# A MoE tail routed in two halves: centred router scores, slots by expert and rank, first rows gathered as products end

## What is computed

```python
x = x + (gelu(h2 @ w1 + b1) @ w2 + b2)      # end of the second stage
hidden = _layernorm(x)                      # (x - m) / sqrt(v + eps)
router_logits = hidden @ w_router           # 512 x 8
top_w, top_i = top_k(router_logits, 2)
top_w = softmax(top_w)
for ei in range(8):
    hmid = silu(hidden @ w0[ei]) * (hidden @ w1[ei])
    out = out + gating[:, ei:ei + 1] * (hmid @ wo[ei])
x = x + out
```

## Time and profile before

| | |
|---|---|
| time, 3 runs | 670.28 us median (668.91 to 671.87) |
| the profiled execution | 669.52 us, span 666.9 us |
| PE busy | 637.5 us (96%) |
| DVE, ACT, POOL busy | 414.5, 371.1, 245.4 us |
| mean granted TensorE clock | 0.991 of full |
| PE's share of the chain that ended last | 78% |

### The profile page before, as it was taken

How to read it: one execution, slowest core, us unless ns; L and a number is a source line. 1 busy time by engine, 2 the same in 40 slices (tenths; PEclk the granted TensorE clock), 3 DMA queues, 4 the chain that set the end, 5 groups by cost and what they waited for, 6 DMA issues and landing times.

```text
span 666.9 us, 10258 instructions
## 1 busy us (share of the span) xinstructions
PE 637.5 (96%) x3720; PEld 525.0 (79%) x3721; DVE 414.5 (62%) x691; ACT 371.1 (56%) x523; POOL 245.4 (37%) x170
## 2 busy tenths in 40 slices
PE   8989999999989999889999999699999999999994
PEld 8867888888867888767888887577888888888883
DVE  7775767658667455567794446661882735753766
ACT  4589998979963344431332443322882736745750
POOL 4059986879883132250000050160022020220233
PEclk9999999999999999999999999789999999999999
DMA  9515544452222413230265962138696573991915
GB/s 327 209 64 198 198 159 166 139 169 96 93 80 71 188 63 128 94 99 31 70 246 157 408 235 77 54 126 300 232 374 228 164 276 118 348 377 45 354 69 184
DMA packets 51846, 116.98 MB, mean 175 GB/s; under 512 B 5208, under 2 KB 5208, under 8 KB 48736
## 3 DMA queue, kind: packets, MB, share of 16 engines
q1 hardware_dynamic: 47360, 106.51, 45.5%
q10 hardware_dynamic: 3168, 5.77, 2.6%
q0 software_dynamic: 1280, 4.20, 1.9%
HBM read 102.31 MB, written 14.16 MB: 175 GB/s over the span
## 4 chain that ended last, share of the span: by engine, by line
PE 78%; DVE 7%; issue 5%; POOL 4%; ACT 4%; DMA 1%; SPq 0%; DVEq 0%; ACTq 0%; POOLq 0%
PE bank L1391 19%; PE bank L1392 18%; PE bank L1393 18%; PE bank L1405 5%; PE bank L1456 3%; POOL nat_lo L478 3%; PE bank L1457 2%; PE bank L1424 2%; PE bank L1425 2%; POOL slots_x L538 1%; PE bank L1819 1%; ACT nat_hi L595 1%; PE bank L1441 1%; PE bank L1632 1%; ACT ct_hi L562 1%
## 5 line engine op out<-in xcount | busy, mean ns | idle before, releaser
L478 POOL TENSOR_TENSOR nat_lo<-raw,nat_hi 128x512 fp32r<-128x512 f32 x104 | 136.2, 1347 | 42.3 <-ACT nat_hi L595 42.1
L526 POOL TENSOR_TENSOR e_lo<-e_raw,e_hi 128x2048 fp32r<-128x2048 f32 x9 | 41.6, 4620 | 221.5 <-ACT e_hi L751 221.5
L871 DVE TENSOR_TENSOR ct_lo<-bank,ct_hi 128x512 fp32r<-128x512 f32 x96 | 65.9, 689 | 33.3 <-ACT ct_hi L562 32.5
L1391 PE MATMUL bank<-w_hi,turned 128*128 128x512 f32 x176 | 70.1, 398 | 1.5 <-DVE turned L1309 1.4
L1393 PE MATMUL bank<-w_hi,turned 128*128 128x512 f32 x176 | 68.7, 391 | 0.0
L1392 PE MATMUL bank<-w_lo,turned 128*128 128x512 f32 x176 | 68.7, 391 | 0.0
L595 ACT ACTIVATE nat_hi<-raw 128x512 fp32r<-128x512 f32 x104 | 64.7, 630 | 0.0
L562 ACT ACTIVATE ct_hi<-bank 128x512 fp32r<-128x512 f32 x96 | 56.9, 596 | 9.0 <-PE bank L1405 6.8
L1391 PE MATMUL bank<-e_hi,turned 128*128 128x512 f32 x144 | 59.0, 409 | 1.5 <-issue 1.5
L1405 PE MATMUL bank<-ident,raw 128*128 128x128 f32 x384 | 57.7, 273 | 0.3
L1392 PE MATMUL bank<-e_lo,turned 128*128 128x512 f32 x144 | 56.9, 395 | 0.0
(11 more groups left out here) (257 smaller groups left out, 1426.2 us busy)
## 6 DMA issues: line engine op xcount, KB each, us to landing
raw<-in_ctx_dram SPq DMA_DIRECT2D x24, 1024.0 KB, 5.0
w_raw<-in_L_ffn_w_dram SPq DMA_DIRECT2D x24, 1024.0 KB, 5.3
e_raw<-in_L_ffn_wo_dram SPq DMA_DIRECT2D x16, 1024.0 KB, 8.0
w_raw<-in_L_attn_w_dram SPq DMA_DIRECT2D x8, 1024.0 KB, 5.2
e_raw<-in_L_ffn_w_dram SPq DMA_DIRECT2D x8, 1024.0 KB, 7.8
slots_x<-zeros SPq DMA_DIRECT2D x1, 4096.0 KB, 15.9
slots_y<-zeros SPq DMA_DIRECT2D x1, 3840.0 KB, 25.6
vectors<-slots_x ACTq DMA_DIRECT2D x11, 256.0 KB, 5.0
```

The costliest lines, as they stand in the source:

```text
L478: nc.gpsimd.tensor_tensor(nat_lo[:, j, :], raw[b % 2][:, j, :], nat_hi[:, j, :].bitcast(f32), ALU.subtract).then_inc(nat_lo_ready, 1)
L526: nc.gpsimd.tensor_tensor(e_lo[j][:, :, :], e_raw[j][:, :, :], e_hi[j][:, :, :].bitcast(f32), ALU.subtract).then_inc(e_lo_ready[j], 1)
L871: nc.vector.tensor_tensor(ct_lo[:, n % CR, :], src, ct_hi[:, n % CR, :].bitcast(f32), ALU.subtract).then_inc(t_lo, 1)
L1391: nc.tensor.matmul(dst, lh, rh, start=first and k == 0, stop=False)
```

## The change

1. The router's weights are centred (each column's mean over the 512 inputs is taken out, by 4 matmuls and one DVE instruction in the eighth feature step, `n == 8` and `n == 9`), so scores come from the unnormalised `xt`; `gap` is multiplied by `rstd` afterwards.
2. Tiles 0 and 1 are turned, scored, picked and ranked between the products of tiles 2 and 3. The picks use DVE's `max` (top 8) twice. `keep_busy` adds 5 matmuls on PE.
3. Expert 0's first rows are gathered tile by tile, in four PSUM banks, and split in four pieces.
4. A slot is expert * 512 + rank, known without the counts of other experts. `slots_x` and `slots_y` grow from 16 and 15 blocks to 32 each. Which 128 rows a block reads is looked up in `place_of`: ACT and SP read it into a register (`row_of`) for each load and store. The zero fills and the router's load move ahead in SP's queue.
5. POOL splits unit 1 of expert 0; DVE splits unit 0 in two halves between gelu steps, and unit 5 of the last expert.
6. `in_last`, its turn and the gates move into the last block, and so does `gathered_added(0)`.

```diff
@@ SP
+            sp.dma_start(w_router[:, :, :], ins["L0_ffn_w_router"].rearrange("(k p) e -> p k e", p=P)).then_inc(router_loaded, 16)
             for u in range(RING, NU):
                 sp.wait_ge(*lower(u - RING))
                 load_w(u)
+                if u in (9, 10):
+                    sp.wait_ge(fixed_ready, 1)
+                    sp.dma_start((xs, ys)[u - 9].rearrange("(n p) d -> p n d", p=P),
+                                 zeros[:, :].unsqueeze(1).to_broadcast([P, ROWS, D])).then_inc(slots_zeroed, 16)
@@ POOL
-        POOL_FIRST = (4, 5)
+        POOL_FIRST = (4, 5, 1)
-            pool.wait_ge(slots_ready, 1)
-            for k in range(2):
-                for t in range(NT):
+            for t in range(NT):
+                pool.wait_ge(slots_ready, t // 2 + 1)
+                for k in range(2):
                     nc.gpsimd.indirect_dma_start(xs[:, :], bass.IndirectOffsetOnAxis(ap=slot_of[k][:, t:t + 1], axis=0),
@@ ACT
+            def row_of(b):
+                return act.value_load(place_of[0:1, bass.ds(b, 1)], min_val=0, max_val=ROWS - 1)
             def load_rows(b):
-                nc.scalar.dma_start(xg, xs[bass.ds(b * P, P), :]).then_inc(xg_loaded, 16)
+                nc.scalar.dma_start(xg, xs[bass.ds(row_of(b) * P, P), :]).then_inc(xg_loaded, 16)
@@ DVE, order from the last gelu step on
+            for t in range(2):
+                second_sum(t)
+                final_stats(t)
+            for t in range(2):
+                final_norm(t)
+            top_two((0, 1))
+            second_sum(2)
+            final_stats(2)
+            rows_of_first(0, 2)
+            final_norm(2)
+            second_sum(3)
+            final_stats(3)
+            passed(picked_and_ranked(0))
+            passed(own_terms(0))
+            passed(own_sums(0))
+            slots_taken(0)
+            top_two((2, 3))
...
+            rows_of_first(2, 4)
...
+            slots_taken(2)
+            for k in range(KD):
+                first_lower_rows(k)
...
+            nc.vector.tensor_tensor(blocks[:, 0, :], upto_extra[:, :], extra[:, :], ALU.subtract).then_inc(slots_ready, 1)
             nc.vector.tensor_copy(blocks[:, 1, :], upto_extra[:, :]).then_inc(slots_ready, 1)
+            split_e(0, 2)
...
+            nc.vector.tensor_scalar(place_of[:, 1:NB + 1], skipped, float(ROWS - 1), None, ALU.min).then_inc(slots_ready, 1)
             split_e(0, 3)
+            link(nc.vector.tensor_scalar(rel_all[:, :, :], slotf_all[:, :, :], last_start[:, 0:1], None, ALU.add))
@@ PE
+                    if t == 2 and n == WHOLE:
                         pe.wait_ge(gelu_ready, FF // P)
                         final_turned(0)
+                    if t == 2 and n == WHOLE + 2:
+                        final_turned(1)
+                        routed(0)
+                    if t == 2 and n == WHOLE + 3:
+                        routed(1)
+                    if t == 3 and n == WHOLE + 2:
+                        ranked_early()
+                        final_turned(2)
...
+            routed(2)
             final_turned(3)
+            first_rows(0)
+            routed(3)
+            first_rows(1)
+            keep_busy(3)
+            ranked_late()
+            keep_busy(2)
+            first_rows(2)
+            first_rows(3)
@@ DVE, end
-            gathered_added(0)
             gathered_added(1)
+            gathered_added(2)
             dve.wait_ge(y_hi_ready, 1)
             nc.vector.tensor_tensor(y_lo[:, :], bank[6][:, :], y_hi.bitcast(f32), ALU.subtract).then_inc(y_lo_ready, 1)
-            gathered_added(2)
-            last_added(0)
-            last_added(1)
             gathered_added(3)
-            last_added(2)
-            last_added(3)
+            for t in range(NT):
+                last_added(t)
```

More of the change, by code:

```diff
@@ L822, in expert_block @@
                     silu(b + 1, 0)
+                if last:
+                    act.wait_ge(rank_done, 3)
+                    nc.scalar.activation(in_lastT, bank[7][:, :].rearrange("p (t n) -> p t n", n=P), ACT.Copy).then_inc(gap_exp, 1)
                 act.wait_ge(unit_done[5], b + 1)
@@ new lines, in places, with top_two @@
+            def places(t0):
+                return RANK_BANK[t0 // 2][:, 0:2 * E].rearrange("p (t e) -> p t e", e=E)
+            counts = RANK_BANK[1][:, 2 * E:3 * E]
+            def top_two(tiles):
+                dve.wait_ge(logits_done, tiles[-1] + 1)
+                for t in tiles:
+                    last = nc.vector.max(top8[:, t, :], score(t))
+                link(last)
+                for t in tiles:
+                    last = nc.vector.scalar_tensor_tensor(second[:, t, :], score(t), top8[:, t, 1:2], pref[:, :], ALU.is_ge, ALU.mult)
+                link(last)
+                for t in tiles:
+                    last = nc.vector.scalar_tensor_tensor(key[:, t, :], score(t), top8[:, t, 0:1], second[:, t, :], ALU.is_equal, ALU.add)
+                link(last)
+                for t in tiles:
+                    last = nc.vector.max(key8[:, t, :], key[:, t, :])
+                link(last)
+                for t in tiles:
+                    nc.vector.tensor_scalar(chosen[:, t, :], key[:, t, :], key8[:, t, 1:2], None, ALU.is_ge).then_inc(chosen_ready, 1)
@@ new lines, in rows_of_first, with mark @@
+            def rows_of_first(t0, t1):
+                dve.wait_ge(chosen_ready, t1)
+                dve.wait_ge(rank_done, t1 // 2)
+                link(nc.vector.tensor_tensor(lane_rank[:, t0:t1], places(t0)[:, :, 0], chosen[:, t0:t1, 0], ALU.mult))
+                for t in range(t0, t1):
+                    nc.vector.tensor_scalar(in_first[:, t, :], lane[:, :], lane_rank[:, t:t + 1], None, ALU.is_equal).then_inc(in_first_ready, 1)
+            def mark(ins_):
+                steps[0] += 1
+                ins_.then_inc(dve_step, 1)
+                return steps[0]
@@ new lines, in passed, with picked_and_ranked, own_terms @@
+            def passed(step):
+                dve.wait_ge(dve_step, step)
+            def picked_and_ranked(t0):
+                two = slice(t0, t0 + 2)
+                for k in range(2):
+                    nc.vector.tensor_tensor(pick[k][:, two, :], key[:, two, :], key8[:, two, k:k + 1].to_broadcast([P, 2, E]), ALU.is_equal)
+                return mark(nc.vector.tensor_tensor(rank[:, two, :], places(t0), base[:, :].unsqueeze(1).to_broadcast([P, 2, E]), ALU.add))
+            def own_terms(t0):
+                two = slice(t0, t0 + 2)
+                return mark(nc.vector.tensor_tensor(scr2[:, :, two, :], rank[:, two, :].unsqueeze(1).to_broadcast([P, 2, 2, E]),
+                                                    picks[:, :, two, :], ALU.mult))
@@ new lines, in _ @@
+            apart = mark(nc.vector.tensor_tensor(gap[:, :], top8[:, :, 1], top8[:, :, 0], ALU.subtract))
+            final_norm(3)
+            passed(apart)
+            nc.vector.tensor_tensor(gap[:, :], gap[:, :], rstd[:, :], ALU.mult).then_inc(gap_ready, 1)
+            rows_of_first(2, 4)
+            more = mark(nc.vector.tensor_scalar(extra[:, :], counts, float(P), None, ALU.is_gt))
+            ranked_ = picked_and_ranked(2)
+            passed(more)
+            more = mark(nc.vector.scalar_tensor_tensor(extra[:, :], counts, float(2 * P), extra[:, :], ALU.is_gt, ALU.add))
@@ L1328, in expert_block @@
                 hidden(b, 0)
+                if last:
+                    for t in range(NT):
+                        half = nc.vector.tensor_scalar(in_last[:, t, :], lane[:, :], rel[0][:, t:t + 1], None, ALU.is_equal)
+                    link(half)
                 lower_hidden(b, 0)
+                if last:
+                    for t in range(NT):
+                        whole = nc.vector.scalar_tensor_tensor(in_last[:, t, :], lane[:, :], rel[1][:, t:t + 1], in_last[:, t, :],
+                                                               ALU.is_equal, ALU.add)
+                    whole.then_inc(chosen_ready, 1)
                 split(0)
@@ L1637, in _ @@
                 u = 2 + n // 4
+                if n == 8:
+                    pe.wait_ge(order_ready, 4)
+                    pe.wait_ge(router_loaded, 16)
+                    for k in range(KD):
+                        mm = nc.tensor.matmul(bank[6][:, 0:E], ones[:, :], w_router[:, k, :], start=k == 0, stop=k == KD - 1)
+                    mm.then_inc(mean_done, 1)
                 if n % 4 == 0:
```

297 lines of the change are left out of this document (154 added, 143 removed).

## The result

The changed kernel takes 665.62 us (median of 5 runs, 664.46 to 667.25), the kernel before beside it 670.28 (668.91 to 671.87): ratio 0.9938, 95% interval 0.9919 to 0.9957. The profiled spans are 662.7 and 666.9 us, a gain of 4.2 where the prediction had 7.3. The gain is real and inside the range, but 3 us of it are missing, so the question is where they went.

The account below looks back on a forecast made before the run. PE, busy 96% of the span, was taken as the bound. Terms -7.1 + 0.95 - 1.15 = -7.3 against 669.52 gave 662.2, taken as 662.6 for the median; forecast 660.5 to 664.5 (chance 0.58), range 659 to 667.

Parts of the forecast that it names:

- the low clock: Rival, chance 0.18: PE's clock stays low in the new routing and gather stretch; about 3 us, 665 to 666.5.
- Mechanism of the stretch: Dense FFN's end to block 1's rows: PE's waits on DVE and low clock go; -7.1 us, first up product 8.6 sooner.
- DVE sets the first turn of `hidden`: Block 0: PE ready at 439.3 waits 2.4 us for DVE and turns at 441.7, 6.8 us sooner.
- DVE is quicker: Rival, chance 0.10: register loads run under the split, PE's 439.3 decides; 2.4 us more gain, 660.
- Block 1's rows hidden: Block 1's rows land at 442.5 to 443.4, ahead of PE's need at 444.9: 1.5 us to spare.
- Centring +0.95: Features stage: four centring matmuls add 0.95 us on PE; DVE's part under 1 us beside idle time.
- The lock on `rstd`: Routing's start: POOL's unit 1 split might hold DVE's small `rstd` instruction, losing about 0.7 us.
- Register loads: Looped blocks: two more loads per block on ACT, 0.35 us each taken, nothing on the path below 1.5 each.
- Fills: Zero fills of 16.8 MB, moved earlier, land by 328 and cost nothing, with 15 us to spare.
- Tail -1.15: Kernel's end: tile 0's additions ahead of the last low part -1.5, DVE's split of the last expert's unit +0.35 us.
- what it adds elsewhere: Step on costs outside the new stretch: centring +0.95 us, fills nothing, register loads nothing on the path.

Follow-up runs that it names:

- e12: e9 with DVE's four small constants instructions spread over features 8 to 11 and `rel_all` ahead of unit 3's last split; 660.14 us, 0.9835 of the kernel before.
- e11: Kernel before with the router's weights loaded early and four centring matmuls in feature 8, result unread; 672.73 us, one run.
- e9: Changed kernel, new tiles on top, expert units moved 448 bytes, dense tiles 512 up, centring moved into a PE wait; 661.75 us, 0.9870 of the kernel before.
- e2: Kernel before with one unused tile of 576 bytes per partition in the place of the change's three new tiles; 673.23 us, ratio 1.0056.
- e3: Changed kernel with the two zero fills issued late, behind the loads of units 4, 5 and 3 of expert 0; 679.15 us, 1.0147 of the kernel before.
- e10: Changed kernel with tile 0's gathered additions behind the last low part, as before the change; 666.73 us, 0.9948 of the kernel before.
- e8: Changed kernel with POOL, not DVE, splitting unit 5 of the last expert again; 667.01 us, 0.9952 of the kernel before.
- e5: Changed kernel with its three new tiles allocated last, so the dense layer's tiles stand where they stood before; 662.06 us, 0.9876 of the kernel before.
- e4: Changed kernel without the five extra `keep_busy` matmuls; 665.54 us, 0.9937 of the kernel before.

## Why the prediction was right, and where its terms were off

The time, 665.62 us, lies in the range of 659 to 667, but outside the forecast of 660.5 to 664.5. It falls where the prediction had put the low clock (665 to 666.5), and the clock was full: that the range held is in part luck, since its width was meant for another case than the one that came.

- **Mechanism of the stretch: right; size 0.7 us less.** Predicted -7.1 to block 1's rows, measured -6.36. The first up product was to come 8.6 us sooner. From the last gelu to it the changed kernel takes 24.35 us (410.91 to 435.26) and the kernel before 32.53, so it comes 8.2 us sooner. The clock stays full and the four old waits are gone.
- **DVE sets the first turn of `hidden`: right; the visible wait is split.** The prediction had PE at the turn at 439.3 and waiting 2.4 us for DVE. The wait on DVE is 0.66 us, because PE stands 1.49 us earlier for its own reading of the block ranges, for which the prediction had no term; together 2.15. The DVE side was the 2.31 us, and 2.25 came. (The prediction's 438.5 + 2.31 makes 440.8 and not 441.0, a slip of 0.2 us.) That this cost hides under the split was the rival "DVE is quicker", and e12 shows the condition: no wait may stand behind the split. That rival was priced at 2.4 us, and e12 got 0.7, since PE's own 1.48 us remain.
- **Block 1's rows hidden: right.** SP's load goes out at 443.50, PE turns at 449.43 without a wait.
- **Centring +0.95: right** (0.95 by e11, given back by e9 in the features, though not in its time). DVE's part beside it was called under 1 us beside idle time; two of its instructions are casts, one met POOL's split, and the feature steps behind it are 0.3 us longer. The prediction had the earlier trace rows for exactly this, and looked for it in another place.
- **The lock on `rstd`: it did not come.** The sub-case, priced at 0.7 us, is refuted by the row at 415.58: 0.15 us, while POOL's split runs from 413.48 to 418.09. What the split does hold back is POOL's own root of tile 0, which starts at 418.04; that costs nothing, since PE turns the unnormalised `xt`.
- **Register loads: 0, right.** Blocks take 193.81 us (193.96). **Fills: 0, right for the dense layer (e2, e3), open for the 0.6 us of the rest.** The fills' old place would cost 12 us now (e3), so "nothing" holds for their new place only.
- **Tail -1.15: right, -1.44 measured.** The order is worth 1.48 (e10), the split on DVE costs 0.22 where 0.35 was said. The larger effect was not in the prediction: DVE's split lets the gathers start 4.3 us sooner, without which the new order would have been 1.9 us slower than the old (e8).
- **Not in the prediction: the place of the tiles.** +2.0 us up to the last gelu by the profiled runs (e2, e5), 3.4 (e2) and 3.6 us (e5) between medians. The step that failed is "what it adds elsewhere", which went through instructions, DMAs and register loads and took every matmul that the diff doesn't touch for unchanged.

The sum: -6.36 - 0.15 - 1.44, + 0.95 for centring, + 0.3 for the cast, + 0.6 for the rest, + 2.0 for the tiles = -4.1, and 4.2 was measured. e5, the change without the shift of tiles, has a median of 662.06 us, where the forecast stood at 662.6; that is closer than the terms deserve, since the profiled runs show 5.8 us (spans of 661.1 and 666.9) where 7.3 was forecast.

e12 beats both kernels: 660.14 us, 0.9835 of the time before, against 0.9938.

## What to carry to other kernels

Read a diff for what it allocates, too: 576 bytes in front of other tiles slowed matmuls that nobody had changed, and an idle tile in the kernel before is a one-line experiment that shows it. When small DVE instructions are moved, ask what POOL does at that time: here casts and 128-wide `tensor_scalar` waited until its split, of 4.6 to 5.0 us, was over. Ahead of a loop whose bounds are read from memory, put the last wait in front of the last long instruction, so that the loop's entry runs under it; here that gave 0.7 us.

## What the runs showed that I had not expected

- The interval of a 128x128x512 matmul depends on where its operands lie in SBUF: steps of 24 take 5.44 us with the dense tiles shifted by 0 or 512 bytes, 5.55 with 576 or 640.
- While POOL splits, a one-element `TENSOR_SCALAR` of DVE takes 0.15 us (not held), but a cast of 8 columns took 3.01, one of 128 columns 1.59 (0.22 alone), and four 128x128 `TENSOR_SCALAR` 4.63 (0.86 alone).
- A loop's entry costs DVE 2.25 us behind a wait and 0.35 when it can run under a split of 2.28 us.
- From the moment the block ranges are ready, PE's next matmul comes 2.5 us later, behind the reads and the loop's entry. With the ranges ready 1.98 us behind the start of the first up product, 1.49 us of it show as idle time; with the ranges 4.95 us ahead of it, none did.
- The clock stayed full through idle times of 0.78 and 0.73 us (e4), in a stretch where PE works between them.
